# Routing of the last but one batch behind the output projection, and block 0's rows loaded ahead of the experts' pieces

## What is computed

```python
def _L0_xattn_ref(x, context, ...):
    ctx_img, ctx_txt = context[:, :257], context[:, 257:]
    q = rms_norm(linear(x, q_w, q_b), norm_q_w)            # 16 heads of 32
    k, v = rms_norm(linear(ctx_txt, k_w, k_b), norm_k_w), linear(ctx_txt, v_w, v_b)
    k_img, v_img = rms_norm(linear(ctx_img, k_img_w, k_img_b), norm_k_img_w), linear(ctx_img, v_img_w, v_img_b)
    out = attention(q, k, v) + attention(q, k_img, v_img)
    return linear(out, o_w, o_b)
def _L0_ffn_ref(x, W1, b1, W2, b2, W3, b3, Wg, bg):
    gate_weights = softmax(x @ Wg + bg); topv, topi = top_k(gate_weights, 2)
    h = gelu(x @ W1[n] + b1[n]); h = gelu(h @ W2[n] + b2[n]); eo = h @ W3[n] + b3[n]   # per expert n
    return sum over the two chosen experts of eo * weight
x = x + _L0_xattn_ref(_layernorm(x), ctx_2048, ...)
x = x + _L0_ffn_ref(_layernorm(x), ...)
```

## Time and profile before

| | us |
|---|---|
| median of 3 runs | 869.69 |
| lowest and highest | 866.67 and 873.19 |
| the profiled execution's own time | 870.31 |
| its span in the profile | 868.5 |

### The profile page before, as it was taken

How to read it: one execution, slowest core, us unless ns; L and a number is a source line. 1 busy time by engine, 2 the same in 40 slices (tenths; PEclk the granted TensorE clock), 3 DMA queues, 4 the chain that set the end, 5 groups by cost and what they waited for, 6 DMA issues and landing times.

```text
span 868.5 us, 17362 instructions
## 1 busy us (share of the span) xinstructions
PE 767.1 (88%) x5934; PEld 668.7 (77%) x5934; DVE 603.7 (70%) x1276; ACT 495.2 (57%) x1131; POOL 231.2 (27%) x286
## 2 busy tenths in 40 slices
PE   3879898999999999764299999999999999999991
PEld 2657676767776767543299999999999999999991
DVE  5476878787878787657166768676767767676853
ACT  4366777777777777682044645554555455454640
POOL 3232334343433333104710303021111112030301
PEclk9999999999999999665599999999999999999996
DMA  6631001020202010405845565656665657565663
GB/s 217 251 135 55 22 38 53 39 65 27 66 26 72 20 43 3 180 21 220 300 157 194 212 216 194 255 174 251 212 247 175 250 198 259 179 246 187 222 213 125
DMA packets 28929, 130.68 MB, mean 150 GB/s; under 512 B 4316, under 2 KB 4332, under 8 KB 17872
## 3 DMA queue, kind: packets, MB, share of 16 engines
q1 hardware_dynamic: 23264, 114.26, 37.3%
q0 software_dynamic: 5616, 15.81, 5.1%
HBM read 113.14 MB, written 19.01 MB: 152 GB/s over the span
## 4 chain that ended last, share of the span: by engine, by line
PE 72%; DVE 11%; ACT 7%; issue 5%; DMA 1%; POOL 1%; SPq 0%; ACTq 0%; DVEq 0%; POOLq 0%
PE tiles L1040 7%; PE tiles L1042 7%; PE tiles L1041 7%; PE scores L1304 4%; PE scores L1302 4%; PE scores L1303 4%; PE ptb L1150 4%; PE ptb L1040 3%; PE ptb L1041 3%; PE ptb L1042 3%; PE pvb L1042 3%; PE pvb L1040 3%; PE pvb L1041 3%; PE pvb L1173 2%; PE scores L1140 2%
## 5 line engine op out<-in xcount | busy, mean ns | idle before, releaser
L834 DVE TENSOR_TENSOR w<-scr,w 128x2048 fp32r<-128x2048 f32 x76 | 174.1, 2291 | 69.9 <-ACT w L624 69.9
L624 ACT ACTIVATE w<-scr 128x2048 fp32r<-128x2048 f32 x76 | 144.8, 1907 | 60.7 <-PE scores L1304 59.3
L470 POOL DMA_INDIRECT out_dram<-scr,tok x18 | 36.5, 2030 | 301.1 <-DVE scr L1030 298.4
L606 ACT ACTIVATE scr<-scr,rsum 112x257 f32<-112x257 f32 x128 | 66.4, 519 | 62.8 <-DVE rsum L818 62.7
L1040 PE MATMUL tiles<-c,w 128*128 128x256 f32 (+1 forms) x272 | 81.3, 299 | 18.1 <-DVE c L722 15.5
L1042 PE MATMUL tiles<-w 128*128 128x256 f32 x288 | 81.5, 283 | 0.0
L1041 PE MATMUL tiles<-w 128*128 128x256 f32 x288 | 81.5, 283 | 0.0
L1040 PE MATMUL tiles<-w 128*128 128x256 f32 x288 | 81.5, 283 | 0.0
L1150 PE MATMUL ptb<-ident,scr 112*128 112x112 f32 x384 | 65.2, 282 | 18.3 <-ACT scr L614 16.6
L1042 PE MATMUL tiles<-c,w 128*128 128x256 f32 (+1 forms) x272 | 78.7, 289 | 0.0
L1041 PE MATMUL tiles<-c,w 128*128 128x256 f32 (+1 forms) x272 | 78.7, 289 | 0.0
(11 more groups left out here) (214 smaller groups left out, 2291.4 us busy)
## 6 DMA issues: line engine op xcount, KB each, us to landing
scr<-in_dram SPq DMA_DIRECT2D x86, 1024.0 KB, 4.8
scr<-in_dram SPq DMA_DIRECT2D x8, 750.0 KB, 4.6
scr<-slots_d SPq DMA_DIRECT2D x10, 528.0 KB, 3.7
slots_d<-rows SPq DMA_DIRECT2D x8, 528.0 KB, 11.6
xn<-in_dram SPq DMA_DIRECT2D x10, 256.0 KB, 3.1
xb<-in_dram SPq DMA_DIRECT2D x8, 224.0 KB, 2.9
xr<-in_dram SPq DMA_DIRECT2D x8, 224.0 KB, 2.5
out_dram<-x SPq DMA_DIRECT2D x8, 224.0 KB, 2.8
```

Source lines behind the costliest of these rows:

```text
L606: act.activation(probs[0:L, s, 0:IMG], probs[0:L, s, 0:IMG], ACT.Copy, scale=rsum[0:L, g, s, 0:1]).then_inc(S["normal_img"], 1)
L624: act.activation(EH[slot], raw[slot], ACT.Copy).then_inc(S["eh_done"], 1)
L834: dve.tensor_tensor(EL[slot], raw[slot], EH[slot].bitcast(F32), ALU.subtract).then_inc(S["el_done"], 1)
```

## The change

Three things are moved.

1. In the last body the routing of batch 6 goes behind the output projection of batch 7: `rank(6)` from step 3 to 6 on TensorE, `gate_weights`, `gate_choice` and `gate_slots` from steps 1, 2, 3 to 4, 4, 7 on VectorE, `scatter(6)` from step 4 to 8 on GpSimd. Of the three converts of steps 2, 3 and 8 only one stays there, at step 9; those of pieces 1 and 2 go behind the routing of batch 7.
2. SP loads block 0's rows `xs` directly behind piece 3 (before: behind pieces 3 to 7). Pieces 4 to 7 of a block are now loaded in that block's own turn of SP's loop, then pieces 0 to 3 of the next block, and last the next block's rows (before: its rows first, then its eight pieces). The 16 fills go from ahead of `add_block(0)` into it, behind its two gathers. The wait for `added` at the end of SP's loop goes.
3. In VectorE's loop the split of the piece in slot 3 goes from pc 7 of the block before to pc 0 of its own block, ahead of the one that stands there. Step 7 has none.

```diff
--- before.py
+++ after.py
@@ -341,53 +341,44 @@
             sp.wait_ge(S["pv_ready"], NC * B)
-            for pc in range(3, PIECES):
-                if pc >= 4:
-                    sp.wait_ge(S["eh_done"], pc - 3)
-                    sp.wait_ge(S["el_done"], pc - 3)
-                sp.dma_start(raw[pc % 4], experts[0, pc]).then_inc(raw_in[pc % 4], 16)
+            sp.dma_start(raw[3], experts[0, 3]).then_inc(raw_in[3], 16)
             sp.wait_ge(scattered[0], 32 * (B // 2))
             sp.wait_ge(scattered[1], 32 * (B // 2))
             sp.dma_start(xs, slots_d[0:BLOCK, :].rearrange("(t p) d -> p t d", p=P)).then_inc(S["xs_in"], 16)
-            sp.dma_start(b3s[:, :], b3[0:1, :].rearrange("e d -> (e d)").partition_broadcast(P)).then_inc(S["b3_in"], 16)
+            sp.wait_ge(S["slots_done"], 1)
             used = sp.value_load(ebi[0:1, MAX_BLOCKS + 1:MAX_BLOCKS + 2], min_val=1, max_val=MAX_BLOCKS)
             with sp.Fori(0, MAX_BLOCKS) as j:
                 with sp.If(j < used):
+                    here = sp.value_load(ebi[0:1, bass.ds(j, 1)], min_val=0, max_val=E - 1)
+                    for pc in range(4, PIECES):
+                        if pc == PIECES - 1:
+                            sp.wait_ge(S["y_sb"], j + 1)
+                            sp.dma_start(b3s[:, :], b3[bass.ds(here, 1), :].rearrange("e d -> (e d)").partition_broadcast(P)).then_inc(S["b3_in"], 16)
+                        sp.wait_ge(S["eh_done"], PIECES * j + pc - 3)
+                        sp.wait_ge(S["el_done"], PIECES * j + pc - 3)
+                        sp.dma_start(raw[pc % 4], experts[bass.ds(here, 1), pc].rearrange("a p n -> (a p) n")).then_inc(raw_in[pc % 4], 16)
                     e = sp.value_load(ebi[0:1, bass.ds(j + 1, 1)], min_val=0, max_val=E - 1)
                     row = sp.value_load(rowi[0:1, bass.ds(j + 1, 1)], min_val=0, max_val=E * REGION - BLOCK)
+                    for pc in range(4):
+                        sp.wait_ge(S["eh_done"], PIECES * j + pc + 5)
+                        sp.wait_ge(S["el_done"], PIECES * j + pc + 5)
+                        sp.dma_start(raw[pc], experts[bass.ds(e, 1), pc].rearrange("a p n -> (a p) n")).then_inc(raw_in[pc], 16)
                     sp.wait_ge(S["filled"], 16 * FILLS * E)
                     sp.wait_ge(S["xT_ready"], j + 1)
                     sp.wait_ge(S["share_set"], 2 * j + 2)
                     sp.dma_start(xs, slots_d[bass.ds(row, BLOCK), :].rearrange("(t p) d -> p t d", p=P)).then_inc(S["xs_in"], 16)
-                    for pc in range(PIECES):
-                        if pc == PIECES - 1:
-                            sp.wait_ge(S["y_sb"], j + 1)
-                            sp.dma_start(b3s[:, :], b3[bass.ds(e, 1), :].rearrange("e d -> (e d)").partition_broadcast(P)).then_inc(S["b3_in"], 16)
-                        sp.wait_ge(S["eh_done"], PIECES * j + pc + 5)
-                        sp.wait_ge(S["el_done"], PIECES * j + pc + 5)
-                        sp.dma_start(raw[pc % 4], experts[bass.ds(e, 1), pc].rearrange("a p n -> (a p) n")).then_inc(raw_in[pc % 4], 16)
-                    sp.wait_ge(S["added"], 32 * (j + 1))
-                    sp.sem_inc(S["held"], 1)
...
@@ -451,6 +442,16 @@
                 taken(pool, ("v1", "v2")[i], n - 2)
                 pool.tensor_copy(c_part(cH)[i], cr[:, :, PARTS[i]]).then_inc(S[("ch0_done", "ch1_done")[i]], 1)
+            def fill_overflow():
+                pool.wait_ge(S["zeroed"], 3)
+                pool.wait_ge(S["fill_ready"], 1)
+                for t in range(FILLS):
+                    for e in range(E):
+                        pool.indirect_dma_start(
+                            out=slots_d, out_offset=bass.IndirectOffsetOnAxis(ap=fillu[:, t, e:e + 1], axis=0),
+                            in_=rows[:, 0, :], in_offset=None).then_inc(S["filled"], 16)
             def add_block(j):
                 e = pool.value_load(ebi[0:1, j:j + 1], min_val=0, max_val=E - 1)
@@ -464,6 +465,8 @@
                         out=sofar_out[:, t, :], out_offset=None, in_=rows_out,
                         in_offset=bass.IndirectOffsetOnAxis(ap=tok[:, t:t + 1], axis=0),
                         bounds_check=T - 1, oob_is_err=False).then_inc(S["gathered"], 16)
+                if j == 0:
+                    fill_overflow()
                 for t in range(2):
                     pool.wait_ge(S["row_done"], 2 * j + t + 1)
@@ -500,7 +503,7 @@
                             pool.wait_ge(S["small_in"], 64)
                         pool.wait_ge(S["xr_in"], 16 * b)
                         pool.tensor_tensor(xr[0:L, :], xr[0:L, :], obr[0:L, :], ALU.add).then_inc(S["xr_ob"], 1)
-                    if h == 4 and has_route(b):
+                    if h == (8 if fixed(b, DONE) else 4) and has_route(b):
                         if fixed(b, FIRST + 2):
                             pool.wait_ge(S["zero_stored"], 16 * E)
                         scatter(b - 2)
@@ -530,13 +533,6 @@
             pool.wait_ge(S["zeroed"], 2)
             pool.tensor_copy(rows[:, 0, D:D + 1].bitcast(U32), far[:, :]).then_inc(S["zeroed"], 1)
             scatter(LAST)
-            pool.wait_ge(S["zeroed"], 3)
-            pool.wait_ge(S["fill_ready"], 1)
-            for t in range(FILLS):
...
@@ -945,17 +941,16 @@
                     if h == 15 and has_prep(b + 1):
                         ln_apply(b + 3, xb[0:L, :], xb, mv1, rs1, "ln1", "xn_done")
                         split_ctx_low(b + 3, 0)
-                    if h == 1 and has_route(b):
+                    if h == (4 if fixed(b, DONE) else 1) and has_route(b):
                         gate_weights(b - 2)
-                    if h == 2 and has_route(b):
+                    if h == (4 if fixed(b, DONE) else 2) and has_route(b):
                         gate_choice(b - 2)
-                    if h == 3 and has_route(b):
+                    if h == (7 if fixed(b, DONE) else 3) and has_route(b):
                         gate_slots(b - 2)
                     if h == 12 and fixed(b, DONE):
                         table_constants()
-                    if fixed(b, DONE) and h in (2, 3, 8):
-                        convert((2, 3, 8).index(h), (2, 3, 8).index(h))
+                    if fixed(b, DONE) and h == 9:
+                        convert(0, 0)
                     if h == 0 and fixed(b, FIRST):
                         dve.wait_ge(S["small_in"], 64)
                         dve.wait_ge(S["zero_stored"], 16 * E)
@@ -1003,9 +998,11 @@
                 dve.wait_ge(S["xTh_done"], j + 1)
                 dve.tensor_tensor(xTL, xTb[:, :, :].rearrange("p b (c n) -> p (b c) n", n=BLOCK), xTH.bitcast(F32), ALU.subtract).then_inc(S["xTl_done"], 1)
-            convert(3, 3)
+            convert(1, 1)
+            convert(2, 2)
             dve.sem_inc(S["hl_done"], 4)
+            dve.sem_inc(S["y_sb"], 1)
             split_input(0)
             used = dve.value_load(ebi[0:1, MAX_BLOCKS + 1:MAX_BLOCKS + 2], min_val=1, max_val=MAX_BLOCKS)
             with dve.Fori(0, MAX_BLOCKS) as j:
@@ -1025,11 +1022,15 @@
                             dve.wait_ge(S["b3_in"], 16 * (j + 1))
                             dve.tensor_tensor(ys, yb[:, :, :], b3s[:, :].unsqueeze(1).to_broadcast([P, 2, D]), ALU.add).then_inc(S["y_sb"], 1)
                             dve.wait_ge(S["gathered"], 32 * (j + 1))
-                            dve.wait_ge(S["y_sb"], j + 1)
+                            dve.wait_ge(S["y_sb"], j + 2)
                             for t in range(2):
                                 dve.scalar_tensor_tensor(ys[:, t, :], ys[:, t, :], share[:, t:t + 1], sofar_out[:, t, :],
                                                          ALU.mult, ALU.add).then_inc(S["row_done"], 1)
-                        convert(PIECES * j + pc + 4, pc % 4)
+                        if pc == 0:
+                            convert(PIECES * j + 3, 3)
+                        if pc < PIECES - 1:
+                            convert(PIECES * j + pc + 4, pc % 4)
                         if pc == 5:
                             split_input(j + 1)
@@ -1216,7 +1217,7 @@
                         for c in range(NC):
                             mm = pe.matmul(pvb[0:L, 0:E], xt[:, c, :], wgs[:, c, :], start=(c == 0), stop=(c == NC - 1))
                         mm.then_inc(S["gate_ready"], 1)
-                    if h == 3 and has_route(b):
+                    if h == (6 if fixed(b, DONE) else 3) and has_route(b):
                         pe.wait_ge(S["a_done"], NC * b)
                         rank(b - 2)
                     for name, lo, hi in FILL[h]:
```

More of the change, by code:

```diff
@@ L364, in _ @@
                     sp.dma_start(xs, slots_d[bass.ds(row, BLOCK), :].rearrange("(t p) d -> p t d", p=P)).then_inc(S["xs_in"], 16)
-                    for pc in range(PIECES):
-                        if pc == PIECES - 1:
-                            sp.wait_ge(S["y_sb"], j + 1)
```

(23 more changed lines are left out.)

## The result

The changed kernel takes 860.83 us (median; the kernel before 870.3 beside it), a ratio of 0.989 with an interval of 0.986 to 0.991. It was timed in two more sets of runs: 861.82 beside 869.31 (0.9895, 0.986 to 0.993) and 860.24 beside 869.74 (0.990, 0.987 to 0.993). The forecast was 863.0, with 857.5 to 869 around it.

The account below looks back on a forecast made before the run. TensorE, busy 88% of the span, was taken as the bound, its gap between the stages as the gain: 870.31 - 10.6 + 5.0 (splits) - 1.9 (end) = 862.8, stated as 863.0 us, range 857.5 to 869.

Parts of the forecast that it names:

- The projection: Between the stages: batch 7's output projection follows the attention directly, gaining 3.1 us; the later scatter 6 costs about 0.1.
- Rival (e): Between the stages: late scatter 6 holds up scatter 7 by all of the 3.1 us, 866; chance 0.03.
- The two landings: Ahead of block 0: scatter 7 lands in 3.1 us, gaining 2.2, and the rows' load in 3.7, gaining 5.4.
- Rival (b): Ahead of block 0: scatter's landing stays 5.3 us and the rows take 6, so 867.3; chance 0.07.
- Tile 7's lateness: In each block the extra split makes tile 7 late: 0.5 us for eight blocks, 1.0 for block 0, +5.0 us.
- Rival (a): Within a block: tile 7 is not late, the 5.0 us shrink to 0 to 2, 857.8 to 859.8; chance 0.20.
- Block 0: First expert block: 1.0 us longer from the late tile beside the fills; TensorE's half clock kept at 6 us.
- Block 1's rows: Next block's rows load: expected to land in 5 to 5.5 us, before the turn, costed at nothing.
- rival (c): Ahead of every turn: rows land late; at 6.4 us 866.8, chance 0.12; at 9.1 us 888.4, chance 0.06.
- Rival (d): In block 0: fills lock VectorE for a whole issue of 0.93 us per op, 6 us more, 869; chance 0.02.
- The end: Last output scatters: without a convert beside them both take 1.01 us, -1.9 us; what follows the last stays 10.9.

Follow-up runs that it names:

- e7: Kernel before with only SP's new load order and the moved fills; routing, converts and the step 7 split as before: 859.33 us, ratio 0.988.
- e11: The changed kernel itself, run again in another set: 860.24 us, ratio 0.990.
- e1: Changed kernel with slot 3's split at the head of pc 0, ahead of tiles 0 to 3: 864.07 us, ratio 0.990; repeated on another chip, 865.61, 0.988.
- e5: The changed kernel itself, run again in another set: 861.82 us, ratio 0.9895.
- e12: Changed kernel with slot 3's split back at pc 7 and pieces 1 to 3 split behind the routing: 860.56 us, ratio 0.987.
- e8: Changed kernel with the 16 fills issued four at a time behind ScalarE's pieces: 870.69 us, ratio 1.001.
- e6: Changed kernel with slot 3's split at the head of pc 0 and the 16 fills issued four at a time: 867.84 us, ratio 0.9975.
- e4: Changed kernel with the 16 fills directly behind scatter 7, ahead of add_block(0), SP's order staying new: 871.76 us, ratio 0.998.
- e10: Changed kernel with slot 3's split back at pc 7 and pieces 1 to 3 split behind the routing: 871.39 us, ratio 0.998.

## Why the prediction was right

The time, the sign and the main terms held. Two of the terms have the right size on a reading that the traces correct, and part of the closeness is luck.

- **The projection** came directly behind the attention (395.36 = 394.01 + 1.35). Forecast -3.1 + 0.1 with scatter 6; e7 against the changed kernel (e11) shows -3.35 (29.13 to 25.78). Rival (e) falls: 1.4 us of wait for the slots were left.
- **The two landings** were forecast at -7.6. e7, which has them alone, shows -7.58. Their sizes came from medians over the whole span, 3.1 and 3.7. Rival (b) falls. But the first of the two, 2.2 us, is not the scatter's landing alone. SP's queue was held by the split of piece 3 until 415.8 in any case, and the wait for the scatter behind that was 0.3 us: a scatter that landed in 3.1 us, in SP's old order, would have gained 0.3 us and not 2.2. The gain came because part 2 took away both holders at once, the wait ahead of piece 7 by the new order, and the late landing. For the second, 5.4 us, one piece by itself is not enough (5.4 to 5.7 us in later blocks); what else made it was not separated.
- **Tile 7's lateness** was forecast at 0.5 us a block and measured at 0.54 (46.90 to 46.35); e1 proves its cause. This was the term with the thinnest margin, 0.35 us by the bare ends. The 0.2 us that were added from the end of a VectorE op to its matmul are not what the trace shows: tile 7's subtraction ends at 535.71, and the weight load that it frees starts at 535.76. The rest of the 0.54 us is made up by tile 6, for which chunk 6 waited 0.1 us, and by the first matmul behind each of the two waits, 0.22 us long for 0.12. So the lateness is as foreseen and the last 0.2 us of it right by luck. Rival (a) falls.
- **Block 0** was forecast 1.0 us longer and came out 0.5 longer. It is made of other things than I said. e7 shows it 1.23 shorter without parts 1 and 3: the half clock lasted from the first expert matmul at 424.4 only to 427.5, some 3 us, where I had kept 6. To e7's 40.79 us come tile 7's half microsecond and the 1.2 us of waiting in front of turn 1, which makes the 42.53.
- **Block 1's rows** are the step that failed, though small. I wrote that SP's wait for the fills "holds back the rows of block 1 alone" and costed it, and that load's landing, at nothing. TensorE waited 1.2 us for them here. Two things made it up: SP's queue stood 0.4 us at the wait for the fills, and the load took 6.7 us to land, where those of the later blocks took 5.4 to 5.7. What SP waited for there:

```profile
SPq L372 <- DMA slots_d<-rows,fillu: 0.4, 1, 0.4
```

  The same kernel's other profiles have 1.2 and 6.0 us (e5) and 0.5 and 6.6 (e11). Where the fills come later, their wait is nearly all of it: SP stood 3.8 us in e12, 11.8 in e8 and 13.5 in e6, and TensorE 3.3, 9.5 and 11.2. The later turns had no wait, with landings as forecast, so rival (c) falls.
- **Rival (d)** falls: in block 0 the casts of tiles 4 to 7 took 0.29 to 0.36 us beside the fills. The lock that the Trainium skill describes (SBUF — State Buffer, section "SBUF: two separate sides") agrees with this trace only on the other side: it was GpSimd that lost time. Fills that take 0.97 us alone took 1.9 and 3.0 beside VectorE's converts:

```profile
433.11 4.49 DVE L830 TENSOR_TENSOR w<-scr,w 128x2048 fp32r<-128x2048 f32 x2
```
```profile
434.35 1.90 POOL L451 DMA_INDIRECT slots_d<-rows,fillu  x1 [0.30 <-issue]
436.55 1.90 POOL L451 DMA_INDIRECT slots_d<-rows,fillu  x1 [0.30 <-issue]
```

- **The end** was forecast at -1.9 and measured at -4.2. The issue gave its 1.9. "What follows the last scatter, I leave as it is" was the mis-sized term: 10.9 us became 8.6, all of it in the last scatter's landing (4.5 to 2.1 us). Before, a piece's load ran beside it and now none does; that this is the cause is likely and not separated.

Sum of the misses: -0.3 between the stages (-10.84 for -10.6), -0.5 in block 0, +0.75 in turns 1 to 9 (4.75 for 4.0: eight periods of 0.54, and some 0.4 more in the block behind turn 1), -2.3 at the end. That is -2.3, and 863.0 - 2.3 = 860.7.

What the whole change does not gain over its second part is now plain as well. Beside e7, parts 1 and 3 bring turn 0 forward by 3.35 us, cost 1.8 in block 0 (with the rows' wait) and 4.6 from turn 1 to turn 9, and give 1.9 at the end. Part 3 by itself, e11 beside e12, costs 2.8 us from turn 1 to turn 9 and gives 1.5 in block 0, since e12 waits longer for block 1's rows, and 1.9 at the end. The best versions measured without the crawl, the changed kernel, e7 and e12, lie at 0.987 to 0.990 with overlapping intervals, and these runs do not tell them apart. e1's kernel reached 0.990 and 0.988 although its two profiles crawl; without the crawl it was not measured. Parts 1 and 2 with the fills in e4's place, so that block 1's rows are not held, were not tried.

**What stays open** is the crawl in block 0. It cost 9 to 13 us, beside the changed kernel's 42.5 from turn 0 to turn 1, in six profiles out of two sets, and did not appear in the six of the other two, nor in the first profile of the changed kernel. The changed kernel was never run in a set in which others crawled, so its 0.989 is shown only for sets without the crawl. In those two sets the kernel before took 872.3 and 873.4 us, against 869.3 and 869.7 in the other two, so part of the crawl may strike it too; it has no profile from there.

## What to carry to other kernels

When a landing takes far more than the median of its kind, ask what it queues behind. Moving the load ahead of that gained 7.6 us here, forecast to 0.1. But look at the waits of the issuing queue as well: 2.2 of these us had two holders, and shortening the landing alone would have given 0.3. Work that is moved off the path must be followed to its next reader: the fills left the path to block 0 and came back in the wait for block 1's rows. And a split that is put between a producer's last tiles costs its own lateness in every block; ask whether its old place cost anything at all.

## What the runs showed of the hardware

- In e10 TensorE's instructions started 0.70 us apart or a multiple of it for some 13 us, in its first pass through a loop, with the data ready and the DMA engines busy for 0.70 of the time; the same program on another chip (e12) ran through at full speed. Of instruction fetching the Trainium skill says (Runtime: NRT & Kernel Launch, section "Instruction fetch mechanics") that an engine streams its code by its own DMA queue and that this is mostly hidden. No run here shows whether fetching is what was slow: the page of e1, which crawled, and that of e5, which did not, list the same instruction packets. From 429 to 444 us e10's profile has none at all, and e12's has two, so no packet of instructions was on its way slowly in that stretch.

```profile
q8 instruction: 26, 0.43, 0.2%
```

- The landing of GpSimd's output scatters had a median of 6.7 us with converts and SP's loads beside them, and of 2.8 in the changed kernel; it was 6.0 in e7, where the convert at step 7 stays, and 5.9 in e1, where a convert stands right behind the additions. So most of the drop comes with having no convert beside the scatters (part 3), and the rest with SP's other order (part 2).
- After a wait of 3.3 us TensorE's granted clock in e12 fell to its lower level, 1.2 GHz (0.50 from 460 to 462 us), and that one wait cost 5.1 us in all, the 3.3 and 1.8 in the block that follows.
